# Projections issued one tile earlier, the second read normalised by ScalarE in pairs, and one decoder tile moved from the first write to the multiply stage

## What is computed

```python
def rat_read(res, W, gamma, beta, num_outputs):
    x = res.reshape(b, l, 256, 4)
    y = einsum('blhc,hoc->bloh', x, W)                 # num_outputs rows of 256
    yn = (y - y.mean(-1)) * rsqrt(y.var(-1) + EPS)
    return yn * gamma + beta

def rat_write(res, y, ...):
    o_d, A_B = y @ wod_w.T, y @ wab_w.T + wab_b
    delta = softplus(o_d[..., 256:] @ du_w.T + du_b)
    A_neg = -softplus(A_logit);  A_bar = exp(delta * A_neg)
    B_bar = (A_bar - 1) / (A_neg - SSM_EPS) * B_proj
    return hs * A_full + out * B_full

x = x + attention(layernorm(x))
h = layernorm(x)
q, k, v = rat_read(h, ..., 3);  h = rat_write(h, causal_attention(rope(q Wq), rope(k Wk), v Wv))
g, u    = rat_read(h, ..., 2);  h = rat_write(h, silu(g ctx0) * (u ctx1))
x = x + h
x = x + layernorm(x) @ dequant(qweight, lut4).T + bias
```

## Time and profile before

| | us |
|---|---|
| median of 3 runs (lowest to highest) | 1807.92 (1806.28 to 1808.39) |
| the profiled execution | 1809.05 |
| its span, first to last instruction | 1807.3 |
| mean granted TensorE clock, share of full speed | 0.941 |
| busy: TensorE, VectorE, ScalarE, POOL | 1594.4, 1357.9, 909.9, 578.4 |

### The profile page before, as it was taken

One profiled execution on the slowest core, in us unless ns is written; L12 is line 12 of the kernel. 1 busy time (PEld: TensorE's weight loads), 2 busy tenths in 40 slices (PEclk: granted clock), 3 DMA queues, 4 the chain that ended last, 5 costly groups with the idle time before them and its releaser, 6 DMA issues. The chain is left out here.

```text
span 1807.3 us, 21042 instructions
## 1 busy us (share of the span) xinstructions
PE 1594.4 (88%) x6880; PEld 1051.9 (58%) x6880; DVE 1357.9 (75%) x2078; ACT 909.9 (50%) x1682; POOL 578.4 (32%) x463
## 2 busy tenths in 40 slices
PE   4899999999999999999999988677889766888999
PEld 3466666666666666666666665465456445445444
DVE  7788888888888887887887766784578679568881
ACT  3355554454554555455554544244268876457630
POOL 2246446446445455455455454101110100000000
PEclk9999999999999999999999999888789856798999
DMA  4002101111111111111110010321544200010121
GB/s 182 24 24 59 35 24 58 36 29 54 36 36 47 36 47 36 35 48 35 36 47 24 24 35 12 120 99 44 108 84 57 90 1 0 1 35 1 47 76 41
DMA packets 30963, 84.20 MB, mean 47 GB/s; under 512 B 6006, under 2 KB 7304, under 8 KB 30600
## 3 DMA queue, kind: packets, MB, share of 16 engines
q1 hardware_dynamic: 30856, 82.87, 15.9%
HBM read 70.27 MB, written 12.58 MB: 46 GB/s over the span
## 5 line engine op out<-in xcount | busy, mean ns | idle before, releaser
L518 DVE SCALAR_TENSOR_TENSOR acc<-pj,sc_o,acc 128x1024 f32<-128x1024 f32 x232 | 293.8, 1279 | 89.6 <-PE pj L649 86.1
L628 POOL TENSOR_TENSOR prob<-prob,inv_total 128x512 f32<-128x512 f32 (+3 forms) x256 | 189.6, 745 | 384.7 <-DVE inv_total L560 384.7
L518 DVE SCALAR_TENSOR_TENSOR q_acc<-pj,sc_q,q_acc 128x1024 f32<-128x1024 f32 x224 | 286.3, 1278 | 34.3 <-PE pj L649 29.0
L649 PE MATMUL pj<-ctx_hi,w_o 128*128 128x512 f32 x528 | 237.1, 449 | 25.5 <-ACT spare L407 12.2
L649 PE MATMUL pj<-zT_hi,w_q 128*128 128x512 f32 x512 | 225.4, 440 | 4.1 <-PEq L81 3.1
L649 PE MATMUL pj<-ctx_lo,w_o 128*128 128x512 f32 x528 | 208.0, 394 | 0.0
L461 ACT ACTIVATE prob<-ps,low_max 128x512 f32<-128x512 f32 (+3 forms) x256 | 134.1, 526 | 144.5 <-DVE low_max L553 144.4
L649 PE MATMUL pj<-zT_lo,w_q 128*128 128x512 f32 x512 | 204.4, 399 | 0.0
L703 PE MATMUL ps<-kT,qT 128*128 128x512 f32 (+3 forms) x512 | 185.6, 445 | 10.4 <-ACT prob L461 10.4
L727 PE MATMUL pv<-probT,v 128*128 128x512 f32 (+3 forms) x512 | 169.4, 433 | 0.0
L649 PEld LDWEIGHTS pj<-ctx_hi,w_o 128*128 128x128 f32 x528 | 99.1, 188 | 110.6 <-DVE acc L518 43.1
(11 more groups left out here) (332 smaller groups left out, 3152.6 us busy)
## 6 DMA issues: line engine op xcount, KB each, us to landing
raw_o<-in_w_o SPq DMA_DIRECT2D x33, 512.0 KB, 3.6
raw_q<-in_w_q SPq DMA_DIRECT2D x32, 512.0 KB, 3.6
x_ring<-qk_kept SPq DMA_DIRECT2D x64, 128.0 KB, 5.0
ln_x<-in_x SPq DMA_DIRECT2D x8, 512.0 KB, 7.0
raw_kv<-in_w_k SPq DMA_DIRECT2D x8, 512.0 KB, 3.5
raw_kv<-in_w_v SPq DMA_DIRECT2D x8, 512.0 KB, 4.1
x<-in_x SPq DMA_DIRECT2D x8, 512.0 KB, 7.2
x_kept<-x SPq DMA_DIRECT2D x8, 512.0 KB, 2.9
```

The costliest lines, as they stand in the source:

```text
L518: dve.scalar_tensor_tensor(out=dst, in0=pj[slot][:], scalar=scale, in1=dst, op0=ALU.mult, op1=ALU.add).then_inc(evac_v, 1)
L628: pool.tensor_tensor(prob[:, k % PROBS, 0:w], prob[:, k % PROBS, 0:w], inv_total[:, n:n + 1].to_broadcast([P, w]), ALU.mult).then_inc(norm ...
L649: ins = pe.matmul(pj[slot][:, b * S:(b + 1) * S], lhs, part[:, b * S:(b + 1) * S], start=n == 0, stop=n == 1)
```

## The change

Three things, in `read_attend`, in `Read` with `write_read`, and in the constants of the decoder.

In `read_attend` rounds 0 and 1 are projected at steps 7 and 8 and rotated at the start of steps 8 and 9, ahead of that step's statistics; round 2 is projected ahead of the last `turn_y`, round 3 ahead of the last `project_v`; `high` stands ahead of `copy_y`; the waits for `moved` and `done` go behind the loop.

In `write_read` VectorE no longer normalises the read's outputs. ScalarE does it as an Identity with scale t and bias -mean * t. The roots and the small rate operations are done for tiles 0-1, 2-3, 4-5 together and for 6 and 7 alone (`Y_SPANS`); the normalised outputs are turned and copied by `Y_TURNS`, tiles 5 and 6 both at step 7.

In the decoder tile 3 moves from the first write to the multiply stage, which has tiles 3, 4 and 5, so 24 quarters instead of 16. It turns tile 3 at step 7 and tile 4 at step 12.

```diff
@@ class Read
+    def root_span(self, act, a, b, n):
+        act.wait_ge(self.var_ready, b)
+        act.activation(self.sd[:, a:b], self.mv[:, a:b, :, 1], ACT.Sqrt, bias=self.eps[:]).then_inc(self.sd_ready, 1)
+
+    def rates_span(self, dve, link, a, b, n):
+        dve.wait_ge(self.sd_ready, n + 1)
+        rsqrt_newton(dve, link, self.r[:, a:b], self.sd[:, a:b], self.mv[:, a:b, :, 1], self.t[:, a:b], LN_EPS)
+        dve.scalar_tensor_tensor(out=self.shift[:, a:b], in0=self.mv[:, a:b, :, 0], scalar=-1.0, in1=self.t[:, a:b],
+                                 op0=ALU.mult, op1=ALU.mult).then_inc(self.shifted, 1)
+
+    def normalise(self, act, i, n):
+        act.wait_ge(self.shifted, n + 1)
+        if i >= 2:
+            act.wait_ge(self.yt, self.nb * (i - 1))
+        for o in range(self.n_out):
+            act.activation(self.yn[i % 2][:, o * XH:(o + 1) * XH].rearrange("p (b k j) -> p b k j", b=2, j=32),
+                           self.y_view(i, o), ACT.Identity, bias=self.shift[:, i, o:o + 1],
+                           scale=self.t[:, i, o:o + 1]).then_inc(self.yn_done, 1)
@@ read_attend, tensor
+                if i == NT + 1:
+                    project(2)
                 if i >= 2:
                     if i == 2:
                         pe.wait_ge(tab_done, 4)
                     rd.turn_y(pe, i - 2, before_last=(lambda v=i - 3: project_v(v)) if i >= 3 else None)
-                if i >= NT:
-                    project(i - NT)
+                if NT - 1 <= i <= NT:
+                    project(i - NT + 1)
+            project(3)
             project_v(NT - 1)
-            project(2)
-            project(3)
@@ read_attend, vector
                 if i < NT:
                     residual(i)
+                else:
+                    rope(i - NT)
...
-                if i >= NT:
-                    rope(i - NT)
-                if i == NT + 1:
+                if i == NT:
                     low(0)
@@ read_attend, scalar
                     rd.copy_h(act, i - 1)
+                if i >= NT:
+                    high(i - NT)
...
-                if i == NT:
-                    act.wait_ge(sel_made, 2)
-                    act.wait_ge(moved, 16 * NT)
-                    act.wait_ge(done, NT)
-                if i >= NT:
-                    high(i - NT)
+            act.wait_ge(sel_made, 2)
+            act.wait_ge(moved, 16 * NT)
+            act.wait_ge(done, NT)
             rows(0)
@@ mlp
-        turn_at = {9: 4}
+        turn_at = {7: 3, 12: 4}
@@ constants
-X_TILES, W1_TILES, W2_TILES = (0, 1), (2, 3), (6, 7)
-Q_W1, Q_MLP, Q_W2, Q_END = 16, 32, 48, 64
+X_TILES, W1_TILES, W2_TILES = (0, 1), (2,), (6, 7)
+Q_W1, Q_MLP, Q_W2, Q_END = 16, 24, 48, 64
+Y_SPANS = {2: (0, 2, 0), 4: (2, 4, 1), 6: (4, 6, 2), 7: (6, 7, 3), 8: (7, 8, 4)}
+Y_TURNS = {2: (0,), 3: (1,), 4: (2,), 5: (3,), 6: (4,), 7: (5, 6), 8: (7,)}
-W1_QUARTERS = ((0, 2, 5, 6, 7, 8, 9, 10), (10, 12, 13, 14, 15, 16, 16, 16))
+W1_QUARTERS = ((0, 2, 4, 5, 6, 7, 8, 8), (8, 8, 8, 8, 8, 8, 8, 8))
@@ write_read, tensor
-                if i >= 1:
-                    rd.turn_y(pe, i - 1)
+                for j in Y_TURNS.get(i, ()):
+                    rd.turn_y(pe, j)
@@ write_read, scalar
-            for i in range(NT + 2):
+            for i in range(NT + 1):
                 if i >= 1 and i + 1 < NT:
                     wr.exponent(act, i + 1)
                 if i == 1:
                     wr.soft_log(act, 1)
-                if 1 <= i <= NT:
-                    rd.root(act, i - 1)
-                if i >= 2:
-                    rd.copy_y(act, i - 2)
+                if i in Y_SPANS:
+                    rd.root_span(act, *Y_SPANS[i])
                 if i < NT:
                     rd.copy_h(act, i)
+                if i in Y_SPANS:
+                    a, b, n = Y_SPANS[i]
+                    for j in range(a, b):
+                        rd.normalise(act, j, n)
+                for j in Y_TURNS.get(i, ()):
+                    rd.copy_y(act, j)
@@ write_read, vector
-                if i >= 1:
-                    rd.finish(dve, link, i - 1)
+                if i in Y_SPANS:
+                    rd.rates_span(dve, link, *Y_SPANS[i])
```

More of the change, by code:

```diff
@@ L839, in __init__ @@
         self.st, self.mv = sb(name + "st", [P, NT, n_out, 6]), sb(name + "mv", [P, NT, n_out, 2])
-        self.sd, self.r, self.t = (sb(name + n, [P, NT, n_out]) for n in ("sd", "r", "t"))
+        self.sd, self.r, self.t, self.shift = (sb(name + n, [P, NT, n_out]) for n in ("sd", "r", "t", "shift"))
         self.p_h, self.p_y, self.p_t = p_h, p_y, p_t
-        self.made, self.ht, self.hc, self.ydone, self.var_ready, self.sd_ready, self.yn_done, self.yt, self.yc = (
-            sem(name + n) for n in ("made", "ht", "hc", "ydone", "var", "sdr", "yn_done", "yt", "yc"))
+        (self.made, self.ht, self.hc, self.ydone, self.var_ready, self.sd_ready, self.shifted, self.yn_done, self.yt,
+         self.yc) = (sem(name + n) for n in ("made", "ht", "hc", "ydone", "var", "sdr", "shifted", "yn_done", "yt", "yc"))
     def y_view(self, i, o):
```

## The result

| | before | after |
|---|---|---|
| median of 8 runs (lowest to highest), us | 1808.73 (1801.42 to 1813.19) | 1819.04 (1814.96 to 1828.11) |
| ratio after / before, 95% interval | | 1.0050 (1.0032 to 1.0068) |
| the profiled execution, its span | 1809.05, 1807.3 | 1817.01, 1815.3 |
| mean granted clock | 0.941 | 0.936 |
| busy: TensorE, VectorE, ScalarE | 1594.4, 1357.9, 909.9 | 1598.5, 1348.9, 910.7 |

A forecast was written before the change was run, and what follows sets the result against it. The prediction took a circle through TensorE and ScalarE, not VectorE, to hold the write-read loop. Terms -5.5 - 8.0 + 13.0 + 5.7 = +5.2 on the profiled 1809.05 gave 1814.3, as a median 1813 us; range 1801 to 1820.

The forecast's parts named there:

- D: Multiply stage with three decoder tiles: two turns' gaps of 3.2 and 4.7 us and a longer tail, +5.7 us.
- B: First write with one decoder tile instead of two: fewer ScalarE blends, so the first exponent comes sooner, -8.0 us.
- rival 4: Ring loads behind the first read give nothing back, so A is 0: 1818.6, slower still; chance 0.08.
- A: Tail of the first read: projections issued one tile earlier bring the first maximum sooner, -5.5 us (-3.5 to -6.3).
- The walk: Step-by-step timing of the first read's tail for A; the second projection arrives 7.0 us after products(7), at 1248.3.
- C: Write-read loop with ScalarE normalising: steps alternate 9.3 and 10.7 us and the tail grows, +13.0 us (+9 to +15).
- rival 1: Write-read loop at the upper clock: products take 2.0 us, C -0.7, sum -8.5, 1799, faster; chance 0.08.
- rival 2: VectorE bounds the write-read loop and all it sheds is gained: C -9, sum -17, 1791, faster; chance 0.05.
- Rival 3: A, B and C at their better ends: sum -0.3, 1808, no change; chance 0.27.

The follow-up runs named there:

- the decoder tile alone: Kernel before with only the decoder edits (one tile in the first write, three in the multiply stage): ratio 1.0019, +3.4 us.
- single tiles: Changed kernel with each tile normalised and turned in its own step instead of in pairs: ratio 1.0015, +2.7 us against the kernel before.

## Why the prediction came out as it did

The forecast was +5.2 against the profiled execution, 1813; the medians differ by 9.0 to 10.3, and both profiled executions by 8.0. The signs of the four terms were right, and so were the mechanisms named for them; one term, D, was too small, since it left out a fall of TensorE's clock, and came out above B. The median of 1819.04 lies outside the 1810 to 1816 that had the chance of 0.52 and 1 us inside the whole range of 1801 to 1820. It is nearest to the 1818.6 of rival 4, whose mechanism fell (below), so that number would have been right by luck.

**A, -5.5.** Measured -5.7 in the pair of profiles. One pair proves little here, since this stretch scatters: over all kernels, the four without part A have 110.7 to 118.8 (mean 114.6), the nine with it 107.1 to 111.0 (mean 109.2). That is -5.4; without the longest one (the decoder tile alone, whose profiled execution was 1831.96 us at a mean clock of 0.893) -4.0. The whole gives -8.5 (-11.4 to -5.4). The walk was off in one step: products(7) took 3.71, not 2.45 as in the earlier trace rows, and the second rotation came at 1251.79 - 2.33 = 1249.5 in the time of before, not at 1248.3. This belongs to the change: products(7) took 3.70 to 3.73 in all nine kernels with the part, and 2.00, 2.45, 3.70 and 3.70 in the four without. The rival by which the ring gives nothing back has fallen: the first load left at 1259.16, before 1260, and the first maximum moved with it. That the pair came so near to the forecast is in part chance. Up to products(6), where no edit is, the kernel after had lost 2.0 us (69.5 from the first transposes, before 67.5); products(6) itself then took 2.00 us instead of 3.39, as in no other kernel with the part. Counted from products(6) the first maximum comes after 45.3 us on average without the part (41.3 to 48.2) and 40.4 with it (37.7, in the change, to 41.6), so 4.9 sooner. Whether the 3 us beyond are A's or the attention's, which lasts 147.6 to 155.9 in kernels where it is the same work, isn't settled.

**B, -8.0.** Measured -8.7 in the pair; by the means of nine kernels with it (39.9) and four without (46.1) -6.3. By the means the term was somewhat too large, and its scatter (38.1 to 42.6 with one tile) goes largely with TensorE's clock, which the forecast held constant: the 38.5 us of the change stand at a clock of 0.77 [the windows above], while the late `copy_y`, with the same instructions in it, has

```profile
1417.21:1459.16 41.95, 33.42 (x104) 18.13 (x104) 22.06 (x31) 30.00 (x57) 5.07 (x9) 0.70 0.26 97
```

The mechanism was right: no blends ahead of the table load, no wait for VectorE's rate.

**C, +13.0.** Measured +12.1 in the pair, +11.0 to +11.3 against the 80.5 to 80.8 that all six other kernels with the old loop have, +10.9 alone in the whole. The 79.7 of before is the exception among the old loops: its clock went up for two of the eight tiles, whose products took 2.00 us, and two of its steps were 7.98 and 8.00 instead of 8.57. Step by step: stats(2) 1.3 later, measured 12.77 - 11.52 = 1.25; steps 9.8, 10.7, 9.3, 10.7, 8.6, measured 9.74, 10.58, 9.25, 10.59, 8.57; tail 10.2, measured 1546.71 - 1536.64 = 10.07. The Identity of 128x256, which no row of before showed and which was set between two others at 0.57, took 0.563:

```profile
L941 ACT ACTIVATE r2yn<-w1py,r2shift,r2t 128x256 f32<-128x256 f32 x16 | 7.8, 563 | 4.2 <-DVE r2shift L933 4.1
```

The rivals here have fallen: the products took 3.65 to 3.68 us, at the lower clock (rival 1), and the shed work of VectorE became idle time (rival 2).

**D, +5.7.** This is the term that was mis-sized: +9.5 in the pair. In the whole, mending the turns gave 9.4 us in the change and 9.5 in the change with the late `copy_y` (+1.4 to -8.1), each give or take some 4, so the whole alone can't tell 9.4 from 5.7; the rows can. Of the 3.8 us missing 0.4 is the tail, 5.8 and not 5.4 from the last silu (1616.35) to the last merge's end (1622.1). The rest the forecast didn't have at all, the fall of TensorE's clock: 2.9 in the products behind the gaps (3.13 + 3.51 - 2 x 1.88), and 0.4 in the first gap, 3.64 instead of 3.23, since its last transposes were slow already (1.12 instead of 0.66). The gap of before had no such fall behind it, and from that one row the forecast took a turn's price as its gap alone. Where the clock stayed up, with the same turns, the stage was +5.1 (copy_y late) and +5.4 (single tiles): the +5.7 of the forecast.

**Rival 3**, all at the better end, would have needed B at -10 by mains at the upper clock; B came to -8.7 in the pair, and the shortest such stretch of all profiles (38.1) is 9.0 below before's.

## What to carry over

- Before moving work from a busy engine to an idle one, write down the circle that sets the loop's step (here transposes, copy, products, statistics, some 8.6 us) and ask what the new instruction hangs onto it, and what stands behind it in its new queue. VectorE lost 9 us of work and the loop got 11 to 12 longer.
- An instruction that waits belongs behind the ones that don't. Putting `copy_y` an iteration later gave 4.8 us in the loop, and giving each half tile its own turn, late enough for its merges, and copying it right behind the silu gave 9.4 us, with no operation removed.
- A gap on TensorE costs its length, and at times a stretch at the lower clock behind it. Splitting it into pieces that hide removes both.

## What the runs showed of the hardware

The clock's fall behind a gap isn't decided by the stage's own instructions alone. Each kernel was profiled in one execution, so this is a comparison of kernels that have these instructions in common; but the runs of one kernel differ too: the eight of the change go from 1814.96 us at a mean clock of 0.938 to 1828.11 at 0.931. The granted clock around the first turn of the change, and around the same turn, with the same two waits (1.06 and 0.85 us), in the kernel with the late `copy_y` (columns as in the earlier trace rows; the clock is the third value from the end):

```profile
1574.00:1581.00 7.00, 5.09 (x14) 2.73 (x14) 5.57 (x9) 3.29 (x6) 0.00 (x0) 0.76 0.00 1
```

```profile
1572.00:1579.00 7.00, 5.08 (x18) 2.44 (x17) 5.96 (x9) 3.66 (x6) 0.00 (x0) 1.00 0.00 1
```

Over all profiles, the multiply stages have fourteen stretches of 2.8 to 5.1 us in which TensorE did no more than a turn or half of one; behind six of them the next four products took 3.13 to 3.62 us instead of 1.88 to 1.97, so 1.3 to 1.7 us more (in two of the six the four behind them were slow too, with 2.11 and 2.72), and behind eight, of 3.2 to 4.6 us, they did not. Behind half turns with no wait (0.44 us) it never fell. The same scatter moves the unchanged attention: 147.6 us at a clock of 0.90 in the change, and with single tiles

```profile
1267.58:1423.47 155.89, 139.75 (x865) 85.03 (x865) 100.70 (x182) 90.69 (x135) 16.68 (x12) 0.84 0.37 66
```

That is 8 us between two profiled executions for a stage of the same instructions, as much as the whole change. A stage's gain can be read from one pair of profiles only where, as in the loop (80.5 to 80.8 in six of the seven kernels that share it), it repeats.
